# A graph layer and a gated feed-forward net: features, rankings and turned weights set beside the last edge walk

## The reference

```python
def reference(x, src, dst, edge_weight, L0_gnn_weight, L0_ffn_W, L0_ffn_b):
    # x 8192 x 512; src (sorted by dst), dst, edge_weight: 131072 edges; ffn: 7 layers of 160 x 160
    h = layernorm(x) @ L0_gnn_weight.T
    x = x + segment_sum(edge_weight[:, None] * h[dst], src, 8192)
    z = layernorm(x)
    mask = (z[:, 0] >= 0.5) & (z[:, 1] >= 0.5)
    a_lo, a_hi, b_lo, b_hi = [decode(z[:, o:o + 16]) for o in (64, 80, 96, 112)]   # first entry over 0.5
    op = z[:, 29]
    g = zeros(8192, 8, 160)           # positions 0 and 1 alone are used at the end
    g[:, 0, 0], g[:, 1, 0], g[:, 0, 1], g[:, 1, 1], g[:, :, 30] = a_lo, a_hi, b_lo, b_hi, op
    for i in range(7):
        g = g @ W[i].T + b[i]
        if i < 6: g = relu(g)
    lo, hi = [clip(round(g[:, s, 2]), 0, 15) for s in (0, 1)]
    out = z
    out[:, 128:144] += 2 * one_hot(lo, 16) * mask
    out[:, 144:160] += 2 * one_hot(hi, 16) * mask
    return x + out
```

## Time and profile before

| | us |
|---|---|
| median of 3 runs | 1762.64 (1757.96 to 1767.19) |
| profiled execution | 1770.79 |
| its span, first to last instruction | 1768.9 |
| TensorE matmul busy | 1601.1 (91%) |
| VectorE busy | 1099.5 (62%) |
| POOL busy | 1093.6 (62%) |
| ScalarE busy | 604.3 (34%) |

### The profile page before, as it was taken

One profiled execution on the slowest core, in us unless ns is written; L12 is line 12 of the kernel. 1 busy time (PEld: TensorE's weight loads), 2 busy tenths in 40 slices (PEclk: granted clock), 3 DMA queues, 4 the chain that ended last, 5 costly groups with the idle time before them and its releaser, 6 DMA issues.

```text
span 1768.9 us, 28755 instructions
## 1 busy us (share of the span) xinstructions
PE 1601.1 (91%) x4076; PEld 661.9 (37%) x4077; DVE 1099.5 (62%) x4047; ACT 604.3 (34%) x1354; POOL 1093.6 (62%) x1114
## 2 busy tenths in 40 slices
PE   7999997999989989989998999999999999995995
PEld 4555543333333333333332333333333333332442
DVE  7666575667666876777668766767633333335465
ACT  7777632222222222222222222222234444443341
POOL 1000005777777777777777777777777777775930
PEclk9999998999999999999999999999999999997798
DMA  7333215777777777766776777777777777772334
GB/s 258 116 136 135 89 68 166 206 204 203 200 199 206 201 201 204 202 196 197 201 201 197 206 203 207 201 205 203 206 209 209 208 209 210 208 210 59 132 111 140
DMA packets 121761, 323.87 MB, mean 183 GB/s; under 512 B 20434, under 2 KB 39154, under 8 KB 121586
## 3 DMA queue, kind: packets, MB, share of 16 engines
q0 software_dynamic: 81920, 268.50, 53.4%
q1 hardware_dynamic: 39666, 53.48, 8.8%
HBM read 288.35 MB, written 33.55 MB: 182 GB/s over the span
## 4 chain that ended last, share of the span: by engine, by line
PE 51%; DMA 15%; DVE 13%; POOL 9%; issue 8%; DVEq 3%; ACT 1%; SPq 1%; ACTq 0%
PE psum L1220 30%; DMA region<-h_rows,region 14%; PE psum L1127 12%; POOL region L531 9%; PE psum L1299 4%; DVE region L937 3%; DVE region L846 2%; PE psum L1116 2%; DVEq L937 2%; DVE region L832 2%; DVE region L838 1%; DVE region L840 1%; DVE region L844 1%; PE psum L1267 1%; PE psum L1137 1%
## 5 line engine op out<-in xcount | busy, mean ns | idle before, releaser
L531 POOL DMA_INDIRECT region<-h_rows,region x1024 | 1013.0, 989 | 579.9 <-DMA h_rows<-region 268.1
L1220 PE MATMUL psum<-region 128*128 x2552 | 1204.9, 611 | 109.4 <-DVE region L937 56.3
L1220 PEld LDWEIGHTS psum<-region 128*128 128x128 f32 x2552 | 443.8, 189 | 832.2 <-issue 822.2
L937 DVE SCALAR_TENSOR_TENSOR region<-region 128x128 f32 (+1 forms) x1276 | 444.9, 351 | 388.3 <-PE psum L1220 269.2
L691 ACT ACTIVATE x<-psum 128x512 f32<-128x512 f32 x192 | 114.7, 597 | 772.5 <-PE psum L1220 772.5
L1127 PE MATMUL psum<-region 128*128 128x512 f32 x512 | 230.2, 593 | 0.9 <-ACT region L593 0.9
L846 DVE COPY_PREDICATED region<-region 128x256 f32<-128x256 int32 x407 | 179.5, 441 | 0.0
L674 ACT ACTIVATE psum<-x 128x512 f32<-128x512 f32 x256 | 153.7, 601 | 8.1
L832 DVE TENSOR_TENSOR region<-region 128x128 int32<-128x128 f32 x452 | 128.9, 285 | 24.9 <-ACT region L620 23.4
L844 DVE TENSOR_TENSOR region<-region 128x128 f32<-128x128 f32 x452 | 128.6, 285 | 0.0
L840 DVE TENSOR_TENSOR region<-region 128x128 f32<-128x128 f32 x452 | 128.2, 284 | 0.1
(11 more groups left out here) (151 smaller groups left out, 639.7 us busy)
## 6 DMA issues: line engine op xcount, KB each, us to landing
x<-in_x SPq DMA_DIRECT2D x16, 1024.0 KB, 5.6
h_rows<-region SPq DMA_DIRECT2D x64, 256.0 KB, 2.0
region<-h_rows,region POOLq DMA_INDIRECT x1024, 3.7
out<-x SPq DMA_DIRECT2D x4, 2816.0 KB, 10.8
out<-x SPq DMA_DIRECT2D x8, 640.0 KB, 3.4
region<-in_L_gnn_weight SPq DMA_DIRECT2D x1, 1024.0 KB, 5.5
region<-in_src SPq DMA_DIRECT2D x4, 128.0 KB, 2.3
region<-in_dst SPq DMA_DIRECT2D x4, 128.0 KB, 2.3
```

Of the source, the lines that this page charges most:

```text
L531: pool.indirect_dma_start(gathered[:, (c + 1) % RING, :], None, h_dram, bass.IndirectOffsetOnAxis(ap=dst_i[g][:, i:i + 1], axis=0),).then_ ...
L937: dve.scalar_tensor_tensor(spread[:, slot % SR, :], iota_n[:, bass.ds((tile - (g * T + 1)) * P, P)], src_f[g][:, bass.ds(chunk - (g * NC + ...
L1220: pe.matmul(banks[:, bass.ds(pe.snap(tile_wanted) % AGG, 1), :].rearrange("p t f -> p (t f)"), spread[:, slot % SR, :], gathered[:, bass.d ...
```

## The change

What it does:

- Means, deviations, gain, shift and features are worked out for each quarter by itself (`prepare(h)`, in eight pieces). For quarters 0 to 2 VectorE does one piece behind each build from steps 272, 288 and 304 of the last walk on; quarter 3's follow behind the slot one-hots of quarter 1. POOL no longer normalises. ScalarE takes the deviations when a quarter's last tile is done.
- TensorE ranks quarters 0 and 1 behind steps 284 and 302, VectorE places them behind steps 298 and 316. Quarters 2 and 3 are ranked behind layer 0 of quarters 0 and 1, into another bank.
- The weights of the five layers are turned behind steps 20, 40 to 100 of the last walk, and copied by VectorE ten steps later, not by ScalarE after the walk.
- The features and small tables move to the memory of edge parts 0 to 2, so that they don't collide with the walk. `packed` and `answer` are cleared once VectorE's own builds are done.
- Packs stand behind layers 1 to 4, spreads as before behind 2 to 5. The first spread of a quarter loads all 16 base registers, before its wait, and waits for the placing of a later quarter, whose ranking uses the same bank.
- Within a layer both halves are multiplied with the first ReLU's result and then both with the second's.

The diff, cut to its core:

```diff
-    FIRST_PACK = 2
+    FIRST_PACK = 1
+    FIRST_SPREAD = 2
...
+    LAST = (PARTS - 1) * NS
+    TURN_LAYER = [LAST + 20 + 20 * l for l in range(L - 2)]
+    READ_LAYER = [at + 10 for at in TURN_LAYER]
+    PREPARE = [LAST + NC + (h + 1) * QT for h in range(QUARTERS - 1)]
+    RANK = [PREPARE[0] + 12, PREPARE[1] + 14]
+    PLACE = [at + 14 for at in RANK]
...
             for h in range(QUARTERS):
                 pool.wait_ge(s_mark, h + 1)
-                if h + 1 < QUARTERS:
-                    normalise(pool, h + 1)
...
-            act.wait_ge(s_ev, 2 * T)
+                    if n % QT == QT - 1:
+                        quarter = slice(n + 1 - QT, n + 1)
+                        act.wait_ge(s_ev, 2 * n + 2)
+                        act.activation(all_sd[:, quarter], all_sq[:, quarter], ACT.Sqrt, bias=eps[:, 0:1], scale=1.0 / D
+                                       ).then_inc(s_alldev, 1)
...
+            def read_layer(l):
+                dve.wait_ge(s_fz, 4)
+                dve.wait_ge(s_fwt, l + 1)
+                dve.tensor_copy(fwT[0:GH, :, l, :].rearrange("p h (s e) -> p h s e", s=2)[:, :, :, 0:GH],
+                                turned_layer(l).rearrange("p (h s e) -> p h s e", h=2, s=2)).then_inc(s_fwe, 1)
...
+            def prepare(h):
+                dve.wait_ge(s_alldev, h + 1)
+                dve.tensor_scalar(all_mean[:, t], all_sum[:, t], 1.0 / D, None, ALU.mult).then_inc(s_gain, 1)
+                dve.reciprocal(all_rstd[:, t], all_sd[:, t]).then_inc(s_gain, 1)
+                yield
...
+            def beside_last_walk(at):
+                for l in range(LH):
+                    if at == READ_LAYER[l]:
+                        read_layer(l)
+                if at == PREPARE[0]:
+                    dve.memset(zero_row[:, :], 0.0)
+                    dve.memset(ones_b[:, :], 1.0)
+                    done(dve.memset(upto[:, :], 0.0))
+                for h in range(len(PREPARE)):
+                    if at >= PREPARE[h]:
+                        next(prepared[h], None)
+                for h in range(len(PLACE)):
+                    if at == PLACE[h]:
+                        place_quarter(h)
...
-            dve.wait_ge(s_ev, 2 * T)
+            dve.wait_ge(s_op, PARTS * NS)
+            dve.memset(f_res[:, 1, 0:1], 0.0).then_inc(s_rese, 1)
+            dve.wait_ge(s_rese, 1)
             for cleared in (packed, answer):
-                dve.memset(cleared, 0.0)
+                dve.memset(cleared, 0.0).then_inc(s_x1, 1)
+            dve.wait_ge(s_x1, 2)
...
-            normalise(dve, 0)
-            find_features(0)
-            place_quarter(0)
+            dve.wait_ge(s_done, PARTS * NS)
             slot_hots(0)
-            find_features(1)
             for h in range(QUARTERS):
                 if h + 1 < QUARTERS:
-                    place_quarter(h + 1)
                     slot_hots(h + 1)
+                if h == 0:
+                    for _ in chain(*prepared[len(PREPARE) - 1:]):
+                        pass
+                if h + len(PLACE) < QUARTERS:
+                    place_quarter(h + len(PLACE))
                 if h:
                     add_hots(h - 1)
-                if h + 2 < QUARTERS:
-                    find_features(h + 2)
                 answers(h)
...
             def spread_tiles(h, g):
+                if g == 0:
+                    pe.reg_load(base, starts[0:1, h, 0:QT])
+                    pe.wait_ge(s_place, min(QUARTERS, h + 2 + len(RANK)))
                 pe.wait_ge(s_quarter, h + 1)
-                pe.reg_load(base, starts[0:1, h, g * NT:(g + 1) * NT])
                 at_least(pe, s_spe, h * GROUPS + g)
...
+                    else:
+                        for d in range(2):
+                            pe.wait_ge(s_fa[d], layers)
+                            for e in range(2):
+                                last = pe.matmul(to[e], fwT[:, d, l - 1, rows[e]], act_f[:, (l - 1) % 2, d, :],
+                                                 start=(d == 0), stop=(d == 1))
+                                if d == 1:
+                                    last.then_inc(s_fs[e], 1)
...
-            rank_quarter(0)
             for g in range(GROUPS):
                 pack_tiles(0, g)
+            pe.wait_ge(s_ev, 2 * T)
             for h in range(QUARTERS):
-                pe.wait_ge(s_fwe, LH)
...
-                    if l == 0 and h + 1 < QUARTERS:
-                        rank_quarter(h + 1)
-                    if h and 0 <= l - FIRST_PACK < GROUPS:
-                        spread_tiles(h - 1, l - FIRST_PACK)
+                    if l == 0 and h + len(RANK) < QUARTERS:
+                        at_least(pe, s_spe, max(0, h - 1) * GROUPS)
+                        rank_quarter(h + len(RANK))
+                    if h and 0 <= l - FIRST_SPREAD < GROUPS:
+                        spread_tiles(h - 1, l - FIRST_SPREAD)
```

## The result

| | before | after |
|---|---|---|
| median (five runs each, one chip) | 1759.95 us (1757.96 to 1767.19) | 1751.66 us (1749.83 to 1754.38) |
| ratio of the times | | 0.9946, 95% interval 0.9924 to 0.9969 |
| profiled execution | 1770.79 | 1754.38 |
| its span | 1768.9 | 1752.5 |

The change makes the kernel faster by 8.3 us of the medians, not by 25.5. The time forecast was 1737, the range 1728 to 1749; the measured one lies 2.7 us above its upper end. (Against 1762.64, the median of three runs on which the forecast stood, the gain is 11.0 us.)

A forecast was written before the change was run, and what follows sets the result against it. POOL's gathers bound the walks, then a chain of waits and TensorE's layers the tail. Gains 16.9 - 1.0 + 1.9 + 3.0 + 3.6 + 1.1 = 25.5 us, off 1762.6, gave 1737.1 us; range 1728 to 1749.

The forecast's parts named there:

- The stretch before the first layer: Walk's end to first layer: memsets, features, ranking and placing leave the chain; gain 16.9 us, bounds 15 to 17.5.
- The last walk: Last walk: moved VectorE work slows POOL's gathers slightly, without a stall; cost 1.0 us, bounds 0 to 2.1.
- Rival D: Last walk: VectorE's moved work stops the gathers, 57 us less the rest's 26.5, giving 1793 us; chance 0.02.
- Quarter 0: First pass of layers: with the fourth pack a layer earlier, last copies hide behind layer 5; gain 1.9 us.
- Quarter 1: Second pass: TensorE at the upper clock, placing wait before first spread costing 0.8 us; gain 3.0 us.
- Quarter 2: Third pass: no ranking wait; load of 16 registers visible 0 to 1.5 us, 0.9 taken overall; gain 3.6 us.
- Quarter 3: Last pass, spreads but no packs: nothing moves, gain 0, with -1.5 us as bound for the longer load.
- The interleave: Order of matmuls within each layer: worth nothing, bounds -0.1 to +0.2 us for each of 20 layers.
- The end: Last answers: TensorE's register load now stands before the wait, beside VectorE's work; gain 1.1 us.
- A: Quarter boundaries: clock falls after all, two or three falls costing 9 to 14 us, 1746 to 1751; chance 0.16.
- C: Quarters 1 to 3: new waits, placing or long register loads, cost 3 us each; 1744 to 1746; chance 0.08.
- the signs that the prediction named for being wrong: Gathers over 1.3 us apart near walk's end, clock 0.50 after quarter 0, or spreads over 2 us behind layer 2.

The follow-up runs named there:

- four loads again: Second run of the changed kernel with each spread group loading its own four base registers; 17.1 us from walk to first layer; 1965.21 us, ratio 0.9889.
- POOL waiting: Changed kernel, with POOL starting its scalings of x only after quarter 0's four slot one-hots; 1759.21 us, ratio 0.9965.
- both edits: Changed kernel with four base registers loaded per spread group and POOL's scalings waiting for eight one-hots; 1744.02 us, ratio 0.9890.
- the changed kernel again: Changed kernel, unaltered, on another chip with a second profile; 1754.74 us, ratio 0.9946 to the kernel before.
- the kernel before once more: Kernel before, unchanged, profiled a second time; span 1762.4 us, tail 160.1 us.
- the run with the packs back: Changed kernel with four base registers loaded per spread group, packs behind layers 2 to 5 as before the change; 1970.69 us, ratio 0.9931.
- four loads: Changed kernel, but each spread group loads its own four base registers behind its waits; 1748.85 us, ratio 0.9854 to the kernel before.
- halves not interleaved: Changed kernel with four base registers loaded per spread group, both matmuls of a layer's first half before the second's; 1967.25 us, ratio 0.9926.

## Why the prediction was right and wrong

**The stretch before the first layer: right.** 16.5 us against 16.9 (bounds 15 to 17.5). Memsets in front of the walk's end, one-hots and first pack at once behind it, ScalarE's copies 2.3 us apart. The profile with the early store (17.1 us) shows what this rests on: a gap of 0.8 between groups of copies is a register load, and it was 0.8 only where no large store ran.

**The last walk: right in kind, too low in size.** I took 1.0 us, with 2.1 as bound; it cost some 2.4. From the lines of the gathers (count, min, median and max in ns, first and last start):

```profile
L533 POOL DMA_INDIRECT region<-h_rows,region x254: 942/946/1831, 1274.4 to 1595.7; - x127
```

(1595.7 - 1274.4) / 253 = 1.270 us apart, against 1.260 before; three more profiles with the same work in the walk (POOL waiting, both edits, the changed kernel again) give 1.267, 1.269 and 1.271, and the kernel before once more 1.261. Over 250 gathers 0.01 us each are some 2.4 us. The price per moved microsecond, 2.4 / 30 = 0.08, is that of walk 3 (0.07). The longest gather is 1.83 us, before 1.06 and 1.08. The Trainium skill, SBUF — State Buffer, "SBUF: two separate sides", says that descriptors of POOL's DMAs can't be written while VectorE runs an operation in a two-port mode. The longer gathers agree with that; which of the moved instructions held them up, no run shows. Rival D, that the moved work holds the gathers up by its whole length or more, is excluded: it would be at least 29 us. The 2.4 us are also what lies between the profiles' 10.7 and the medians' 8.3, but with the second profile of before (tail 160.1) it is 8.6 and 8.3, so that this proves nothing.

**Quarter 0: right in sum (2.1 against 1.9), wrong in its reason.** I let ScalarE's idle 2.97 us go because the fourth pack moved. The long gap is still there after (second row below), only one group of copies earlier, where TensorE loses 0.64 us by it and not 3.51. And the run with the packs back, in which no store ran beside these copies any more, has none. Before, the second large store was issued just ahead of ScalarE's register load, in the SP row below that ends at 1659.2 (the load's gap is 1661.68 to 1664.65); after, it was issued by 1628.1, and the gap ends at 1635.13, again within the 10 us that such a store runs. The likeliest reason is therefore the one shown for TensorE, a load beside a store; it was not tried by itself.

```profile
1639.25 19.92 SPq L501 DMA_DIRECT2D out<-x  x2
...
1635.13 1.44 ACT L721 ACTIVATE region<-psum 5x128 f32 x4 [3.00 <-issue]
...
1726.86 0.61 SPq L501 DMA_DIRECT2D out<-x  x1
```

(The first and third row are of before, the second of after.)

**Quarter 1: right.** 3.6 against 3.0: clock 1.00 all through, the wait for the placing 0.76 against 0.8.

**Quarter 2: the step that failed.** It said of the 16 base registers: visible 0 to 1.5, taken 0.9. Measured: 4.63, and then 5.6 more for the clock. The row that I took for 16 registers, VectorE's 1.26, came from a walk in which no store runs; that load also costs 0.35 to 1.67 on TensorE without the store. The other row, 1.49 for four registers, was a load beside the store: that was issued at 1726.86 (third row above), and the load was over at 1733.73 + 1.49 = 1735.22, 8.4 us later. Set side by side, four registers cost more than sixteen, and I should have asked why; what I did was to take them as the two ends of one range. The row of 1.49 alone would have given the bound: four times the registers, 1.49 x 4 = 6.0, and quarter 3 shows 6.03 (near by chance, since its last loads ran after the store).

**Quarter 3: the same step.** It was put at nothing, with -1.5 as bound; measured -6.5, of which 4.5 are the longer gap, and 1.9 the clock. That the clock stays at 1.00 behind a gap of 1.5 us, as before, was wrong by itself: with four loads the gap is 1.55 and the quarter still 1.7 us longer than before. Why, no run shows.

**The interleave: right, nothing** where packs lie between; in quarter 3 the clock hides what it does. **The end: right**, 0.8 against 1.1.

**The rivals.** A (falls of the clock) and C (register loads beside the output's DMAs, 3 us each) each had the right mechanism, and were priced apart: 9 to 14 and some 8. The measured loss is mostly one cause, C's, with A as its consequence: 8.3 us of gaps and 7.5 of clock, of which some 1.7, in quarter 3, came with four loads as well. Two of the signs that the prediction named for being wrong came as well: spreads over 2 us behind layer 2, and a clock at 0.50 behind quarter 0. A range that took either, but not both together, ended 2.7 us too low.

With loads of four the changed kernel came near what was forecast: ratio 0.9854 (0.9827 to 0.9881), 23.3 us below the median of before on that chip, and 0.9889 and 0.9890 in the comparisons of it and of its variant with POOL's wait on other chips (forecast: 1737.1 / 1762.6 = 0.9855). Each is below the 0.9946 of the changed kernel: two of the three intervals lie wholly under it, and the widest (0.9826 to 0.9951) just reaches it. It is faster than the kernel before in all three.

## What to carry to other kernels

A register load on an engine's own queue is work of that engine: several small ones, each hidden by the work queued before it, can be cheaper than one large one, above all where a large DMA runs. When two rows price the same kind of operation and the cheaper is the bigger one, look at what ran beside each before either enters a sum. And where a gap of a few microseconds is possible on TensorE, price it together with the clock behind it: here a gap cost about twice its length.

## What the runs showed of the hardware

- **Register loads from SBUF.** On TensorE, beside a store of 2816 KB, the spread's matmul came 9.5 to 9.7, 12.1 and 14.0 us after layer 0 for 4, 8 and 16 registers, repeatable to 0.2 us; without the store it came after 9.6 us for 16 and after 7.9 at most for 4. On ScalarE four registers took 0.86 us without and 3.03 with a store.
- **The clock behind a short gap.** Behind layer 2 of quarter 3, gaps of 1.49 and 1.41 us were followed by 1.00 throughout in both profiles of the kernel before. Gaps of 1.54 to 1.67 at the same place were followed by a stretch below 1.00 in all six profiles of variants that have them: by 3 to 4 us at 0.50 (four loads again), and by some 17 us (halves not interleaved). Gaps of 4.5 us and more were followed by 0.50 in each of the three profiles that have them. What decides at the short gaps stays open.
- **VectorE beside a stream of POOL's operations.** In one of twelve profiles of the changed kernel and its variants a tensor-tensor operation of 0.69 us took 20.8, with POOL's scalings of x without a pause beside it; in the other eleven the longest took 1.10 to 1.38. The Trainium skill, SBUF — State Buffer, "Who interferes with whom", says that a tensor-tensor operation with both inputs in SBUF and POOL's reads exclude each other; the trace agrees that VectorE can lose. Why it waited through some 25 of POOL's operations that once, no run shows, and a wait that keeps the two apart (both edits) brought no time that could be measured.
